# The value product of the last slot moved ahead of a slot's last two max products

## What is computed

```python
qkv = zn @ w_qkv                                   # zn: the normalised input
scores = jnp.einsum('bhqd,bhkd->bhqk', q, k) / SCALING
att = jax.nn.softmax(scores, axis=-1)
out = jnp.einsum('bhal,bhlv->bhav', att, v)
out = out @ w_proj + b_proj
```

## Time and profile before

| | |
|---|---|
| median of 3 runs | 983.86 us (983.48 to 985.3) |
| profiled execution | 983.9 us, of which the span is 982.1 us |
| PE busy (modelled) | 882.3 us, 90% of the span |
| DVE busy | 792.7 us, 81% |
| ACT busy | 663.7 us, 68% |
| POOL busy | 314.5 us, 32% |
| granted TensorE clock | 0.968 of full speed on average |

### The profile page before, as it was taken

One profiled execution on the slowest core, in us unless ns is written; L12 is line 12 of the kernel. 1 busy time (PEld: TensorE's weight loads), 2 busy tenths in 40 slices (PEclk: granted clock), 3 DMA queues, 4 the chain that ended last, 5 costly groups with the idle time before them and its releaser, 6 DMA issues. The chain is left out here.

```text
span 982.1 us, 14337 instructions
## 1 busy us (share of the span) xinstructions
PE 882.3 (90%) x5188; PEld 319.8 (33%) x5188; DVE 792.7 (81%) x1568; ACT 663.7 (68%) x728; POOL 314.5 (32%) x450
## 2 busy tenths in 40 slices
PE   6879999999999999999999999999989989757985
PEld 3312322222243233322332242322322313136863
DVE  4598879898979878899888879889799788265765
ACT  5128778787877787878877868788677768901110
POOL 4041010005424414139443423255243232822113
PEclk9769999999999999999999999999999989988998
DMA  5631010310320203101411022004310001240001
GB/s 143 105 45 39 16 53 16 73 41 10 90 61 13 93 12 70 38 13 55 89 61 56 12 39 59 23 7 105 91 56 14 11 13 31 85 172 23 1 1 64
DMA packets 52375, 49.08 MB, mean 50 GB/s; under 512 B 17504, under 2 KB 43696, under 8 KB 51920
## 3 DMA queue, kind: packets, MB, share of 16 engines
q1 hardware_dynamic: 51680, 46.91, 19.4%
q0 software_dynamic: 384, 1.05, 0.3%
q10 hardware_dynamic: 240, 0.20, 0.2%
HBM read 18.06 MB, written 9.17 MB: 28 GB/s over the span
## 5 line engine op out<-in xcount | busy, mean ns | idle before, releaser
L1331 DVE TENSOR_REDUCE mx<-ring 128x1 f32<-128x512 f32 x1024 | 633.9, 680 | 110.3 <-PE ring L1038 109.6
L873 ACT ACTIVATE prob<-sc,unscale 128x1024 f32<-128x1024 f32 x512 | 539.1, 1113 | 85.2 <-PE sc L1056 83.9
L1038 PE MATMUL ring<-kp,qp 48*128 48x512 f16 x1024 | 299.4, 395 | 43.5 <-DVE mx L1331 22.5
L1070 PE MATMUL obank<-prob,vaug 128*32 128x512 f32 x2048 | 276.1, 612 | 0.7 <-ACT prob L873 0.6
L1038 PEld LDWEIGHTS ring<-kp,qp 48*128 48x128 f16 x1024 | 74.1, 93 | 361.4 <-DVE mx L1331 301.3
L1056 PE MATMUL sc<-qp,kp 64*128 64x512 f16 x1024 | 167.9, 381 | 14.0 <-ACT prob L873 13.3
L644 POOL TENSOR_TENSOR parts<-qkf,parts 128x1024 f16<-128x1024 f32 x14 | 29.9, 2134 | 209.6 <-ACT parts L803 209.6
L1056 PEld LDWEIGHTS sc<-qp,kp 64*128 64x128 f16 x1024 | 50.4, 95 | 92.3 <-ACT prob L873 83.9
L631 POOL TENSOR_TENSOR hid<-hid,b 128x512 f32<-128x512 f32 x24 | 30.2, 1270 | 110.9 <-ACT hid L827 110.9
L639 POOL TENSOR_TENSOR yA<-yA,sums 128x512 f32<-128x512 f32 x15 | 19.0, 1269 | 131.1 <-DMA sums<-reciprocal_scratch 131.1
L1070 PEld LDWEIGHTS obank<-prob,vaug 128*32 128x32 f32 x2048 | 40.5, 108 | 61.5 <-issue 58.4
(11 more groups left out here) (221 smaller groups left out, 749.2 us busy)
## 6 DMA issues: line engine op xcount, KB each, us to landing
x_sb<-x SPq DMA_DIRECT2D x7, 1024.0 KB, 6.0
kp<-parts SPq DMA_DIRECT2D x48, 128.0 KB, 4.4
qp<-parts SPq DMA_DIRECT2D x93, 64.0 KB, 5.5
out<-hid SPq DMA_DIRECT2D x4, 1024.0 KB, 5.3
yA<-oT SPq DMA_DIRECT2D x124, 32.0 KB
sums<-reciprocal_scratch SPq DMA_DIRECT2D x31, 128.0 KB
x_scratch<-x SPq DMA_DIRECT2D x3, 1024.0 KB, 4.5
qp<-mp SPq DMA_DIRECT2D x128, 2.0 KB
```

The costliest lines, as they stand in the source:

```text
L873: nc.scalar.activation(prob[:, e % 2, 2 * a:2 * a + 2, :].rearrange("p g n -> p (g n)"), sbuf2[a][:, :], ACT.Exp, scale=unscale[:, 0:1]).t ...
L1038: nc.tensor.matmul(dst[:, :], qp[rows, qh, h, qt * P:(qt + 1) * P], kp[rows, h, kh * HALF:(kh + 1) * HALF], start=True, stop=True).then_in ...
L1070: ins = nc.tensor.matmul(obank[i * VW:(i + 1) * VW, :], vaug[:, b % 2, kt, c0:c0 + VW], prob[:, v % 2, i, :], start=(kt == 0), stop=(kt == ...
L1331: nc.vector.tensor_reduce(mx[:, u % 2, n:n + 1], src[:, :], AX.X, ALU.max).then_inc(rv_free, 1)
```

## The change

In the loop over the slots the value product of slot e - 1 now stands ahead of the max products 2 and 3 of slot t, directly behind the scores. No instruction is added or left out, and no semaphore changes.

```diff
@@ -1094,10 +1094,10 @@
                     i = QK_LEAD.index(t)
                     keys_or_queries(sbuf2[i // 2][:, i % 2 * HALF:(i % 2 + 1) * HALF], 2 + i // NH, i % NH)\
                         .then_inc(s_lead, 1)
+                if 0 <= e - 1 < NS:
+                    value_product(e - 1)
                 if t < NS:
                     max_products(range(2, 4))
-                if 0 <= e - 1 < NS:
-                    value_product(e - 1)
 
             last = B - 1
             row = GH * HD
```

## The result

The changed kernel takes 1068.45 us (median of 4 runs, 1067.47 to 1071.88) against 984.5 us for the kernel before (4 runs; the table above has the first three of them). The ratio is 1.086, 95% interval 1.083 to 1.089: slower by 84 us, or 8.6% by the ratio. The profiled execution took 1071.88 us, with a span of 1070.0, the longest of the four, 3.4 us over the median.

What follows compares the result with a forecast made beforehand. The bound was taken to be the hand-over between TensorE and VectorE through three ring banks. Terms 78 - 10 + 0 + 14 + 3 + 1 = +86, less 1, on 983.9 gave 1069, taken as 1068 us; range 1042 to 1088.

Steps and rivals of the forecast that it cites:

- the plain slots: Slots without ring items: period 2.94 us instead of 2.49, +0.45 in 174 slots, +78 us (61 to 90).
- the transposed maxima: 27 slots transposing the maxima, a ring item shifting the banks followers need: +4, +6 and +4 us, bounds 0 to +28.
- The handoff: From a max product's start until the product three later may start: 0.42 + 0.69 + 0.06 = 1.17 us.
- The second part: Rest of the plain slot's loop, from product 1 through scores and value product to products 2 and 3: 1.77 us.
- Which gap: One gap between max products lies on the loop; scores and value product now share it, so the scores' +0.45 us shows.
- Slots with projections: 24 slots with projections but no transpose of the maxima: the gap is split in two, -0.41 us each, -10 together.
- the slots with plain transposes: 10 slots with the transpose of the maxima and only other transposes beside it: 4.32 against 3.69 us, +0.63 each, +6.
- ScalarE's waits: After slots with keys or queries, scores and value product wait for late ScalarE: 0.15 in 12 slots, 0.35 in 3, +3 us.
- A: Rival: TensorE's wait ahead of product 3 is filled and plain slots fall to 2.40 us; 958 us, chance 0.05.
- B: Rival: no difference, since VectorE's own rate sets the slot or TensorE takes products out of order; 984 us, chance 0.03.
- D: Rival: score matmuls overlap product 1's wait, hiding half of the 0.45 us; about 1020 us, chance 0.04.
- C: Rival: more waiting also lowers TensorE's clock in half of the plain slots, 130 us on top; about 1200 us, chance 0.04.

Runs made afterwards that it cites:

- e2: Kernel before, with each slot's first pair of score matmuls issued twice: 988.88 us, against 984.12 for the kernel before run beside it.
- e3: Changed kernel, with each slot's first pair of score matmuls issued twice: 1120.67 us.
- e4: Changed kernel, with each maximum taken over 256 of the 512 columns only: 1001.04 us.
- e1: Kernel before, with the scores moved behind max product 3, directly ahead of the value product: 1095.05 us.
- e5: Changed kernel, with scores moved to the slot's start and ScalarE's ring items behind its exponentials, or between them where there are transposes: 983.75 us.
- e8: Changed kernel, with the transpose of the maxima between its slot's two other ring items instead of ahead of them: 1059.36 us.

## Why the prediction was right

The forecast was 1068 us, and the median is 1068.45. That it is right to half a microsecond is luck: the plain slots came out 4 us under their term, the transposed maxima and slots 13 and 14 some 4 over theirs, and the profiled execution lies 88.0 us above the 983.9 that the sum started from, not 85. The mechanism is not luck; nearly every term was met by its own kind of slot. The chain of steps:

- **The loop, and its length.** The handoff came out at 1.17 as read from the earlier trace rows. The second part I had put at 1.77; it is 1.75, because the value product follows the last score matmul in 0.30 (229.399 to 229.703 in the trace of the changed kernel), where the tail gave 0.32. The first score matmul, put at +0.23 behind product 1, starts beside it (228.957 and 228.953); the last still starts at +0.45, so nothing of the 0.44 was hidden by that and the misreading cost nothing. All this makes 2.92 instead of 2.94 and is most of the 4 us by which the plain term was too large. e2 and e3 confirm that the scores are the difference, e4 that the maximum is in the loop once.
- **Which gap.** e1 and e5 show that it is the sharing of one gap: both pieces together in either gap, 2.92; one piece in each, 2.49.
- **Slots with projections.** -0.44 and -0.41 each, as the sum had it; this is the only gain of the change, and 24 such slots stand against 174 plain ones.
- **The transposed maxima.** The rule (a ring item shifts the bank that its followers need) gave 14 us with no row to show it; 15.6 were measured, and e8 took back 12.7 in these slots by the ring's order alone. Too small was the term for the slots with plain transposes: +0.77 each instead of +0.63, as product 1 is released at 2.70 and not at 2.55: in the trace of the changed kernel ScalarE starts 0.69 us after the first item (301.76 to 302.45) and takes 0.78.
- **ScalarE's waits** (+3) are inside the plain slots' mean, 2.935 against a median of 2.920: 174 x 0.015 = 2.6. They are 9 slots of 3.09 and 3 of 3.25, where 12 and 3 had been counted.
- **The rivals.** A (958 us) needed a full bank when VectorE ran dry; the 0.44 idle in each slot shows that there was none. Both kernels turn through the same three banks, and work put into TensorE's wait didn't make the changed one gain. B and D fall with 2.92. C: the clock held 1.00 with TensorE 671 of 792 us busy, so waits of 0.57 us once a slot don't bring it down here, as the tail had suggested.
- **Not foreseen:** +2.6 us in slots 13 and 14, which the prediction had put at nothing as start-up. They are still at the half clock in the trace (it ends at 82.0 us, at 75.8 in the kernel before), and the value product takes twice as long in the gap. e8's trace shows the same slots at 4.67 us.

By the page's totals the change looked like filling a wait: TensorE had 301 us of waiting for VectorE. The scores were filling part of that wait already.

## What to carry to other kernels

With a ring of buffers between two engines, don't ask how much the producer waits but which gap of its other work lies behind the product that waits. Here, with three buffers and four products a turn, the period is one handoff (produce, consume, hand back) plus the largest gap between successive products, and work in the other gaps is free up to a limit: 0.22 us more of it was. Other numbers of buffers and products close the loop over other gaps; no run here shows them. So spread other work evenly between the products, largest pieces apart; and before an item is moved in the ring's order, count which buffer each follower will then need. When a gap is shortened, look next at the consumer's queue: what stands there in order behind an item that now comes later.

## What the runs showed of the hardware

- A max product on one half of the array's rows and a score matmul on the other start within 4 ns of each other (228.953 and 228.957 in the changed kernel), so product 1, though alone and late, overlaps the first score matmul.
- Four maxima over 256 columns take 1.41 us, four over 512 take 2.48: 0.27 less for each, and the handoff fell by the same 0.27.
- Behind the start-up and up to the last max product the granted clock (1.00 is 2.4 GHz, 0.50 is 1.2 GHz) fell only in the last batch, beside one long wait of TensorE for VectorE. In the kernel before it fell at 714.1 us, behind a wait of 1.51 us, and at 789.2, in a wait of 3.08; in the changed kernel at 873.9, behind one of 1.84; in e1 at 801.9 and 829.2, behind 1.51 and 1.52, and at 890.6, in one of 3.89. Such a wait doesn't always do it: another of 1.51 us, ended at 735.57 in the kernel before, left the clock at 1.00. With waits of 0.57 us once a slot it stayed at 1.00 for 792 us.
